# Row maxima of the first 20 units: adjacent banks, one VectorE reduction per unit

## The chip, the core and the metric

The kernel runs on one core of a Trainium2 chip. The metric is the device time of one execution in microseconds; three runs of the kernel before gave 2825.81, 2823.85 and 2824.11 us (median 2824.11). The engines are named as the profile names them: PE (TensorE), DVE (VectorE), ACT (ScalarE), POOL (GpSimd), SP (SyncE, which issues most DMAs).

## The reference, cut to what matters

Eight sequences of 1024 tokens by 256 channels pass through four residual blocks: a retention layer, a channel mix, a 16-head softmax attention with a relative bias, and the same channel mix again. The part in question is the attention:

```python
scores = jnp.einsum('bhqd,bhkd->bhqk', q, k) / np.sqrt(HEAD_DIM)   # HEAD_DIM = 16
attn = jax.nn.softmax(scores + bias[None], axis=-1)
out = jnp.einsum('bhqk,bhkd->bhqd', attn, v)
```

The kernel subtracts from the scores of each query a number that is close to the row's maximum over all 1024 keys before the exponential, so each sequence needs 16 heads x 1024 queries row maxima.

## The kernel before, in words

One sequence b follows another (the loops `for b in range(B)` in each engine's block). For each, PE runs retention, the first channel mix (q = 0 and 1, the two halves of the tokens), the projections of the attention, and then the attention itself. The second channel mix of sequence b-1 (q = 2 and 3) is laid by hand into the beginning of the attention of sequence b: that is `last_mix_and_rows` on PE (from about L748), with its counterparts on ACT (`last_mix`) and on DVE (the chain of `if u == ...` after `row_max(u)`, about L1830).

**Units.** A unit u is one head and one block of 128 queries; there are NU = 128 of them. Its scores against 1024 keys are two products of 128x512 (L882), k = 0 and 1 for the two halves of the keys. Each fills one PSUM bank (2 KiB a partition), and DVE reduces each to one maximum per query (`row_max`, L1809). After every 16 units a small reduction (L1813) joins the two halves' maxima, PE transposes them (`max_transpose`, L897), ACT negates them (L1435), and DMAs (L462) write them as an extra row of the queries' operand. Only then can the main loop multiply that block the other way round (`score_cols`, L916), with keys as rows, take exponentials (ACT, L1464), multiply the band of the bias (POOL, L2018) and weigh the values (PE, L941).

**Order of the products.** Products are numbered c. For c < 44 (2 * AHEAD, AHEAD = 22) `row_product` gives four products to two units: c = 4m is (unit 2m, k = 0), 4m+1 is (unit 2m+1, k = 0), 4m+2 is (unit 2m, k = 1), 4m+3 is (unit 2m+1, k = 1). `some_rows(1)` issues one row of two products, c = 2r and 2r+1; between the rows of `last_mix_and_rows` stand pieces of the earlier sequence's channel mix (L693, L715, L735). In the first sequence there is no earlier one and the rows follow each other.

**Banks.** For c < 40 the product goes to bank c % 4, later to bank c % 3 (`ROW_BANKS`). `score_rows` makes PE wait, before product c, until DVE has counted in `mx_r` the maximum of the last product in the same bank (`LAST_ROW[c] + 1`). PE's instructions stay in their order, so everything behind that wait waits too. `row_max(n)` makes DVE wait for `mx_s >= c + 1`, the count of finished products, before each of its two reductions.

**DVE's order around the change.** After `row_max(0)` come the statistics of the last layer norm of sequence b-1 (`ln_stats(b - 1, 5)`), after `row_max(2)` its four normalisations (L1628), after 7 and 12 the mixes of the last quarter (L1639), after 9, 10, 18 and 20 the gated outputs (L1649). PE's pieces wait for these: the transposes (L676) for the normalisations, `mix_k(b - 1, 3, ...)` (L693) for the gated output after 9, `mix_r(b - 1, 3, ...)` (L715) for the mixes after 12. When the ahead part ends, u = 22, the main loop `for s in range(NS + LAG)` starts with four more row products and four column products a step; `score_cols` waits once for 40 maxima.

Of the kernel before, what the change touches and what calls it, by code (L numbers as in the profile page):

```python
# [17 lines left out]
ALU = mybir.AluOpType  # L18
ACT = mybir.ActivationFunctionType
AX_X = mybir.AxisListType.X  # L20
# [21 lines left out]
AHEAD = 22  # L42
# [25 lines left out]
def build(nc, ins, out):  # L68
# [10 lines left out]
    NU = HEADS * NT  # L79
    NS = HEADS // 4 * 2 * NT  # L80

    with ExitStack() as ctx:
        def sb(name, shape, dt=F32):
            return ctx.enter_context(nc.sbuf_tensor(name, shape, dt))
# [6 lines left out]
        def tally(owner, name, each, step=1):  # L91
            t = Tally(sem(name), each, step)
            tallies[owner].append(t)
            return t
# [5 lines left out]
        psum = ctx.enter_context(nc.psum_tensor("psum", [P, 8, 512], F32))  # L100
# [62 lines left out]
        mx2 = sb("mx2", [P, 2, 16, 2])  # L163
# [144 lines left out]
        mx_s = tally("pe", "mx_s", 2 * NU)  # L308
        mx_r = tally("dve", "mx_r", 2 * NU)
# [24 lines left out]
        def need(eng, t, b, n):  # L334

            eng.wait_ge(t.sem, t.at(b, n))
# [28 lines left out]
        def unit(u):  # L365

            blk, ii, hh = u // 16, u % 8 // 2, u % 16 // 8 * 2 + u % 2
            return blk // 2 * 4 + hh, blk % 2 * 4 + ii, blk, hh * 4 + ii
# [42 lines left out]
        def row_product(c):  # L411

            if c < 2 * AHEAD:
                return c // 4 * 2 + c % 2, c % 4 // 2
            return c // 2, c % 2

        ROW_BANKS = [c % 4 if c < 2 * AHEAD - 4 else c % 3 for c in range(2 * NU)]
        LAST_ROW = [max((m for m in range(c) if ROW_BANKS[m] == ROW_BANKS[c]), default=None) for c in range(2 * NU)]

        def row_bank(c):  # L420

            return bank[ROW_BANKS[c]]

# [182 lines left out]
        def _(pe):  # L606
# [263 lines left out]
            def score_rows(b, c):  # L870

                u, k = row_product(c)
                h, i, _, _ = unit(u)
                if k == 0:
                    rows_wait(b, u)
                if c == 0:
                    pe.wait_ge(fn_T, 2 * norm_at(b, 3) + 2)
                if c == 3:
                    need(pe, c_lo, b, 8)
                if LAST_ROW[c] is not None:  # L880
                    need(pe, mx_r, b, LAST_ROW[c] + 1)
                pe.matmul(row_bank(c), SQ[rows_of(h, MAX_ROW), h // 2, i * P:i * P + P],  # L882
                          SK[rows_of(h, MAX_ROW), h // 2, 512 * k:512 * k + 512], start=True, stop=True)\
                    .then_inc(mx_s.sem, 1)
# [600 lines left out]
        def _(dve):  # L1485
# [145 lines left out]
            def mixes(b, q, sides=(0, 1), chunks=(0, 1)):  # L1631

                g, n, at = q % 2, norm_at(b, q % 2 + (0, 4)[q // 2]), mix_at(b, q)
                for i in sides:
                    dst, nu = ((xkT, NU_K), (xrT, NU_R))[i]
                    for c in chunks:
                        dve.wait_ge(fn_T, 2 * n + c + 1)
                        dve.wait_ge(mix_a, 4 * at + 2 * i + c + 1)
                        nc.vector.scalar_tensor_tensor(dst[:, c, :], nT[:, c, 512 * g:512 + 512 * g],  # L1639
                                                       vec[:, nu.start + c:nu.start + c + 1], dst[:, c, :],  # L1640
                                                       ALU.mult, ALU.add).then_inc(mix_b, 1)
# [71 lines left out]
            for b in range(B):  # L1713

                for t in range(NT + 1):
# [27 lines left out]
                    if 1 <= t <= NT:  # L1743
# [4 lines left out]
                        if u < NT - 1:  # L1748
                            need(dve, p_st, b, u + 1)
                            for pr in range(2):  # L1750
                                new = bank[6][:, pr * DV:pr * DV + DV]
                                if u == 0:
                                    i = nc.vector.tensor_copy(S[:, pr, :], new)
                                else:
                                    need(dve, s_upd, b, 2 * u + pr - 1)
                                    i = nc.vector.scalar_tensor_tensor(S[:, pr, :], S[:, pr, :], gamma[:, pr:pr + 1],
                                                                       new, ALU.mult, ALU.add)
# [31 lines left out]
                for n in range(8):  # L1789
# [11 lines left out]
                    if n == 7 and b > 0:  # L1801
                        mixes(b - 1, 2, (1,))

                def row_max(n):
                    for c in (2 * n, 2 * n + 1):
                        u, k = row_product(c)
                        _, _, blk, col = unit(u)
                        need(dve, mx_s, b, c + 1)
                        nc.vector.tensor_reduce(mx2[:, blk % 2, col, k:k + 1], row_bank(c), AX_X, ALU.max)\  # L1809
                            .then_inc(mx_r.sem, 1)  # L1810
                    if n % 16 == 15:
                        need(dve, mx_r, b, 2 * n + 2)
                        nc.vector.tensor_reduce(mx[:, blk, :], mx2[:, blk % 2], AX_X, ALU.max).then_inc(mx_f.sem, 1)  # L1813
# [8 lines left out]
                for u in range(AHEAD):  # L1822
                    row_max(u)
                    if b > 0:
                        if u == 0:
                            ln_stats(b - 1, 5)
                        elif u == 2:
                            ln_norms(b - 1, 5)
                        elif u == 7:
                            mixes(b - 1, 3, (0,))  # L1830
                        elif u == 9:
                            gated(b - 1, 2, (0,))
                        elif u == 10:
                            gated(b - 1, 2, (1,))
                        elif u == 12:
                            mixes(b - 1, 3, (1,))
                        elif u == 18:
                            gated(b - 1, 3, (0,))
                        elif u == 20:
                            gated(b - 1, 3, (1,))  # L1840
                u = AHEAD
                for s in range(NS + 4):
                    if s < NS:
                        while u < units[s]:
                            row_max(u)
                            u += 1
# [238 lines left out]
```

## Time and profile before

| | us |
|---|---|
| median of three runs | 2824.11 (2823.85 to 2825.81) |
| the profiled execution, its own time | 2824.51 |
| its span in the trace | 2822.7 |
| PE busy | 2696.9 (96%) |
| DVE busy | 2143.4 (76%) |
| ACT busy | 1741.6 (62%) |
| POOL busy | 1252.9 (44%) |
| mean granted clock of PE | 0.979 of full speed |

The profiled execution took 2824.51 us, 1.8 us more than the span that the trace covers, and 0.4 us more than the median. Busy shares are means over stages that have different limits; the stretches in which the first 20 units are worked on are some 40 us of each sequence's about 345 us. A clock of 1.00 in the profile is 2.4 GHz for PE and 0.50 is 1.2 GHz.

### The profile page before, as it was taken

The page shows a single profiled execution, that of the slowest core. Times are in us where ns is not written, and L with a number is a line of the kernel's source. Part 1 is how long each engine was busy: PE and PEld are TensorE (multiplying, and loading weights), DVE is VectorE, ACT ScalarE, POOL GpSimd, SP SyncE. Part 2 cuts the span into 40 slices and gives each one's busy share as a digit, 9 for nine tenths or more (in the row PEclk, how much of TensorE's full clock was granted, in tenths as well). Part 3 has the DMA queues.
Part 4 walks back from the last instruction along what each step waited for, and adds up shares of the span by engine and source line. Part 5 has one row for each costly group of instructions (what it writes and reads, how often), then busy time and mean ns, then how long its engine had stood idle before and what let it go on. Part 6 is the DMA issues. An engine that isn't in the chain of part 4 may idle for free.

```text
span 2822.7 us, 53686 instructions
## 1 busy us (share of the span) xinstructions
PE 2696.9 (96%) x19682; PEld 1476.0 (52%) x19682; DVE 2143.4 (76%) x4443; ACT 1741.6 (62%) x3671; POOL 1252.9 (44%) x1764
## 2 busy tenths in 40 slices
PE   6989999999999999999999999999999999999998
PEld 5733376433764338643486334854358533575334
DVE  5769856897569966689666996669956799567993
ACT  4428854488544884458744587536874378643885
POOL 3425544255433554335543455434454345433553
PEclk9979999999999999999999999999999999999999
DMA  6150001600015000250002400034000330003300
GB/s 193 31 126 11 24 9 34 146 17 24 9 43 137 17 24 9 57 124 17 31 1 68 113 17 31 1 89 91 17 31 13 97 72 17 31 31 93 59 2 16
DMA packets 71429, 139.18 MB, mean 49 GB/s; under 512 B 12784, under 2 KB 49696, under 8 KB 70016
## 3 DMA queue, kind: packets, MB, share of 16 engines
q1 hardware_dynamic: 69152, 135.29, 19.2%
q8 instruction: 158, 2.59, 0.4%
q14 instruction: 103, 0.84, 0.1%
q10 hardware_dynamic: 2016, 0.45, 0.1%
HBM read 86.02 MB, written 38.82 MB: 44 GB/s over the span
## 4 chain that ended last, share of the span: by engine, by line
PE 70%; DVE 17%; POOL 4%; issue 4%; ACT 2%; SPq 1%; DMA 1%; POOLq 0%; DVEq 0%; ACTq 0%
PE psum L882 18%; PE psum L941 16%; DVE mx L1809 8%; PE psum L655 7%; PE psum L1008 3%; PE psum L659 3%; PE psum L916 3%; PE psum L715 2%; PE psum L1064 2%; PE psum L977 2%; PE psum L842 2%; DVE nrm L1628 2%; POOL X L1926 1%; PE psum L1049 1%; DVE xrT L1639 1%
## 5 line engine op out<-in xcount | busy, mean ns | idle before, releaser
L1809 DVE TENSOR_REDUCE mx<-psum 128x1 f32<-128x512 f32 x2048 | 1265.5, 684 | 81.9 <-PE psum L882 81.1
L1464 ACT ACTIVATE Z<-psum 128x512 f32<-128x512 f32 x2048 | 1110.2, 598 | 273.2 <-PE psum L916 244.6
L2018 POOL TENSOR_TENSOR Z<-Z,W_low 128x256 f32<-128x256 f32 (+1 forms) x1152 | 713.2, 642 | 662.5 <-ACT Z L1464 655.5
L882 PE MATMUL psum<-SK,SQ 63*128 63x512 f32 x2048 | 761.2, 474 | 31.0 <-DVE mx L1809 26.1
L916 PE MATMUL psum<-SQ,SK 64*128 64x512 f32 x2048 | 756.3, 469 | 9.3 <-DMA SQ<-mrow 8.8
L941 PE MATMUL psum<-Z,Vx 128*17 128x256 f32 x8192 | 642.0, 388 | 0.4 <-POOL Z L2018 0.4
L882 PEld LDWEIGHTS psum<-SK,SQ 63*128 63x128 f32 x2048 | 309.0, 190 | 481.3 <-DVE mx L1809 368.0
L916 PEld LDWEIGHTS psum<-SQ,SK 64*128 64x128 f32 x2048 | 309.0, 188 | 81.4 <-ACT Z L1464 37.4
L941 PEld LDWEIGHTS psum<-Z,Vx 128*17 128x17 f32 x8192 | 138.3, 95 | 334.1 <-issue 275.6
L1926 POOL TENSOR_TENSOR X<-X,mixed 128x512 f32<-128x512 f32 x64 | 80.5, 1268 | 274.2 <-DVE mixed L1649 274.2
L1963 POOL TENSOR_TENSOR Z<-Z 128x512 f32<-128x512 f32 x64 | 82.0, 1281 | 244.5 <-DVE Z L1683 244.5
L655 PE MATMUL psum<-W_high,zT_both 128*128 128x512 f32 x384 | 166.2, 433 | 0.5 <-ACT Z L1347 0.5
L655 PE MATMUL psum<-W_low,zT_both 128*128 128x512 f32 x384 | 152.1, 396 | 0.0
L715 PE MATMUL psum<-WT,xrT 128*128 128x256 f32 x512 | 135.2, 409 | 14.0 <-DVE xrT L1639 14.0
L1385 ACT ACTIVATE Z<-psum 128x128 f32<-128x128 f32 x256 | 67.3, 277 | 107.0 <-PE psum L1064 107.0
L693 PE MATMUL psum<-xkT,WT 128*128 128x512 f32 x256 | 126.3, 612 | 5.5 <-DVE mixed L1649 3.1
L1347 ACT ACTIVATE zT_both<-psum,vec 128x128 fp32r<-128x128 f32 x128 | 51.6, 453 | 116.2 <-PE psum L649 115.6
L842 PE MATMUL psum<-nT,WT 128*128 128x512 f32 x256 | 115.8, 600 | 6.9 <-ACT nT L1294 6.6
L715 PEld LDWEIGHTS psum<-WT,xrT 128*128 128x128 f32 x512 | 98.3, 201 | 42.1 <-DVE xrT L1639 16.2
L659 PE MATMUL psum<-W_high,zT_both 128*128 128x512 f32 x384 | 120.0, 394 | 0.0
L1628 DVE TENSOR_SCALAR nrm<-X,fmv,frs 128x256 f32<-128x256 f32 x192 | 77.9, 467 | 43.7 <-POOL frs L1912 43.7
L1320 ACT ACTIVATE mixed<-psum 128x512 f32<-128x512 f32 x64 | 37.9, 594 | 117.2 <-PE psum L715 117.2
(135 smaller groups left out, 3535.9 us busy)
## 6 DMA issues: line engine op xcount, KB each, us to landing
W_low<-bias_rows SPq DMA_DIRECT2D x8, 2048.0 KB, 8.8
parts<-Z SPq DMA_DIRECT2D x32, 512.0 KB
W_low<-low_parts SPq DMA_DIRECT2D x7, 1536.0 KB, 6.7
X<-L_attn_a_x SPq DMA_DIRECT2D x8, 1024.0 KB, 5.7
SQ<-parts SPq DMA_DIRECT2D x32, 256.0 KB, 7.9
SK<-parts SPq DMA_DIRECT2D x32, 256.0 KB, 10.9
SQ<-parts SPq DMA_DIRECT2D x16, 512.0 KB, 6.6
SK<-parts SPq DMA_DIRECT2D x16, 512.0 KB, 14.6
```

What stands on the lines that cost most here:

```text
L655: pe.matmul(bank[dst], zT_parts[0][:, t % 2, c, :], Wqkvg_parts[part][:, c, c0:c0 + 512], start=c == 0 and part == 0, stop=False)
L659: mm = pe.matmul(bank[dst], zT_parts[1][:, t % 2, c, :], Wqkvg_parts[0][:, c, c0:c0 + 512], start=False, stop=c == C - 1)
L693: mm = pe.matmul(k_bank(b, q, o), WT[:, W_K, c, o * P:o * P + P], xkT[:, c, :], start=c == 0, stop=c == C - 1)
L715: mm = pe.matmul(bank[4 + pr][:, i * D:i * D + D], xrT[:, c, t * P:t * P + P], WT[:, W_R, c, :], start=c == 0, stop=c == C - 1)
L842: mm = pe.matmul(bank[QK_BANK[n % 2]], WT[:, A_Q + side, c, h * P:h * P + P], nT[:, c, 1 + 512 * g:513 + 512 * g], start=c == 0, stop=c == ...
L882: pe.matmul(row_bank(c), SQ[rows_of(h, MAX_ROW), h // 2, i * P:i * P + P], SK[rows_of(h, MAX_ROW), h // 2, 512 * k:512 * k + 512], start=T ...
L916: pe.matmul(col_bank(n), SK[rows_of(h), h // 2, j * P:j * P + P], SQ[rows_of(h), h // 2, 512 * half:512 * half + 512], start=True, stop=Tr ...
L941: mm = pe.matmul(sum_bank(s // 8)[32 * c:32 * c + HD + 1, cols], Vx[:, j, 4 * hg + c, :], ring[:, (4 * s + cols_of(s).index(c)) % RING, cols],
L1464: nc.scalar.activation(ring[:, n % RING, :], col_bank(n), ACT.Exp)\
L1628: nc.vector.tensor_scalar(nrm[:, i, :], X_of[b % 2][:, 4 * g + i, :], fmv[:, i, 0:1], frs[:, i:i + 1], ALU.subtract, ALU.mult).then_inc(fn ...
L1809: nc.vector.tensor_reduce(mx2[:, blk % 2, col, k:k + 1], row_bank(c), AX_X, ALU.max)\
L2018: nc.gpsimd.tensor_tensor(ring[:, n % RING, a:z], ring[:, n % RING, a:z], band_exp[:, 4 * hg + cols_of(s)[i], at:at + z - a], ALU.mult)\
```

## The change

For c < 40 the banks are given as 0, 2, 1, 3 by c % 4 in place of 0, 1, 2, 3. With the order of the products unchanged, the two halves of unit 2m then lie in banks 0 and 1, those of unit 2m+1 in banks 2 and 3. DVE reduces the two banks of a unit in one instruction, 128 x 2 x 512 to 128 x 2, and does so for two units at a time: nothing at even n, and at odd n, after a wait for all four products of the pair, the reduction of unit n-1 (adds 1 to `mx_r`) and that of unit n (adds 3). The other statements in DVE's order stay after the `row_max(u)` after which they stood. Units 20 and up are done as before.

```diff
-        ROW_BANKS = [c % 4 if c < 2 * AHEAD - 4 else c % 3 for c in range(2 * NU)]
+        ROW_BANKS = [(0, 2, 1, 3)[c % 4] if c < 2 * AHEAD - 4 else c % 3 for c in range(2 * NU)]
...
+                def two_units(n):
+                    need(dve, mx_s, b, 2 * n + 4)
+                    for i in range(2):
+                        _, _, blk, col = unit(n + i)
+                        nc.vector.tensor_reduce(mx2[:, blk % 2, col, :], psum[:, 2 * i:2 * i + 2, :], AX_X, ALU.max)\
+                            .then_inc(mx_r.sem, (1, 3)[i])
+
                 def row_max(n):
-                    for c in (2 * n, 2 * n + 1):
+                    if n < AHEAD - 2 and n % 2 == 1:
+                        two_units(n - 1)
+                        _, _, blk, _ = unit(n)
+                    for c in (2 * n, 2 * n + 1) if n >= AHEAD - 2 else ():
                         u, k = row_product(c)
                         _, _, blk, col = unit(u)
                         need(dve, mx_s, b, c + 1)
```

## Rows read from the trace of the kernel before

**Rows 1.** The page: the chain that ended last, by engine.

```profile
PE 70%; DVE 17%; POOL 4%; issue 4%; ACT 2%; SPq 1%; DMA 1%; POOLq 0%; DVEq 0%; ACTq 0%
```

**Rows 2.** Windows, ahead part: length, busy PE, PEld, DVE, ACT, POOL; PEclk; DMA.

```profile
1533.00:1578.00 45.00, 41.82 (x157) 22.77 (x155) 39.89 (x70) 13.30 (x23) 9.40 (x9) 1.00 0.56 144
1879.00:1924.00 45.00, 41.92 (x150) 23.16 (x148) 37.44 (x66) 11.11 (x20) 9.40 (x9) 0.92 0.50 133
```

**Rows 3.** Timeline of PE, fifth sequence: start, length, line, count, idle before it.

```profile
1536.90 0.50 PE L882 MATMUL psum<-SK,SQ 63*128 63x512 f32 x2
...
1539.68 2.00 PE L854 MATMUL psum<-WT,nT 128*128 128x256 f32 x8
...
1549.51 0.50 PE L882 MATMUL psum<-SK,SQ 63*128 63x512 f32 x2
1549.93 1.13 PE L715 MATMUL psum<-WT,xrT 128*128 128x256 f32 x4
1550.99 0.49 PE L882 MATMUL psum<-SK,SQ 63*128 63x512 f32 x2
...
1557.18 1.13 PE L693 MATMUL psum<-xkT,WT 128*128 128x512 f32 x2 [0.34 <-DVE mixed L1649]
...
1564.56 1.13 PE L715 MATMUL psum<-WT,xrT 128*128 128x256 f32 x4 [2.00 <-DVE xrT L1639]
...
1575.55 0.73 PE L882 MATMUL psum<-SK,SQ 63*128 63x512 f32 x3
```

**Rows 4.** Timeline of DVE in the same stretch.

```profile
1538.61 1.28 DVE L1809 TENSOR_REDUCE mx<-psum 128x1 f32<-128x512 f32 x2
1539.81 1.39 DVE L1617 BATCH_NORM_STATS2 fstat<-X 128x6 f32<-128x256 f32 x4
...
1541.60 2.45 DVE L1809 TENSOR_REDUCE mx<-psum 128x1 f32<-128x512 f32 x4
...
1550.04 1.29 DVE L1809 TENSOR_REDUCE mx<-psum 128x1 f32<-128x512 f32 x2 [0.20 <-PE psum L882]
...
1577.89 7.26 DVE L1809 TENSOR_REDUCE mx<-psum 128x1 f32<-128x512 f32 x12
```

**Rows 5.** Groups of DVE's instructions by line and shape: busy us, mean ns, idle before.

```profile
L1809 DVE TENSOR_REDUCE mx<-psum 128x1 f32<-128x512 f32 x2048 | 1265.5, 684 | 81.9 <-PE psum L882 81.1
...
L1726 DVE TENSOR_TENSOR Z<-psum,mask 128x512 f32<-128x512 f32 x64 | 44.2, 691 | 22.3 <-PE psum L1055 22.2
...
L1813 DVE TENSOR_REDUCE mx<-mx 128x16 f32<-128x32 f32 x64 | 11.9, 187 | 2.2
...
L1586 DVE TENSOR_REDUCE xrT<-xrT 128x16 f32<-128x512 f32 x1 | 1.0, 994 | 0.0
```

**Rows 6.** Timeline of PE's weight loads second sequence, where PE waits for a maximum.

```profile
542.03 0.18 PEld L882 LDWEIGHTS psum<-SK,SQ 63*128 63x128 f32 x1 [0.99 <-DVE mx L1809]
```

**Rows 7.** Timeline of DVE, second sequence: the reduction that this load waits for.

```profile
540.10 2.48 DVE L1809 TENSOR_REDUCE mx<-psum 128x1 f32<-128x512 f32 x4
```

**Rows 8.** Timeline of PE, sixth sequence, where its clock is low.

```profile
1880.68 0.50 PE L882 MATMUL psum<-SK,SQ 63*128 63x512 f32 x2
...
1908.34 2.07 PE L715 MATMUL psum<-WT,xrT 128*128 128x256 f32 x4 [2.00 <-DVE xrT L1639]
1910.34 0.79 PE L882 MATMUL psum<-SK,SQ 63*128 63x512 f32 x2
...
1922.49 0.73 PE L882 MATMUL psum<-SK,SQ 63*128 63x512 f32 x3
```

**Rows 9.** Timeline of PE, first sequence.

```profile
171.84 1.22 PE L882 MATMUL psum<-SK,SQ 63*128 63x512 f32 x4 [2.15 <-DMA SK<-Z]
...
182.57 0.38 PE L897 MATMUL psum<-ident,mx 128*16 128x128 f32 x1 [0.62 <-DVE mx L1813]
...
197.08 0.79 PE L916 MATMUL psum<-SQ,SK 64*128 64x512 f32 x1 [7.65 <-DMA SQ<-mrow]
```

**Rows 10.** Timeline of DVE, first sequence.

```profile
172.64 9.66 DVE L1809 TENSOR_REDUCE mx<-psum 128x1 f32<-128x512 f32 x16 [1.41 <-PE psum L882]
```

## The prediction

> **What bounds the kernel now.** The page first: PE is busy 96% of the span (the table) and holds 70% of the chain that ended last, DVE 17% [rows 1]. So time is gained or lost where PE stands still; DVE's instructions count only where PE waits for them. Next the windows around the ahead part (the 22 units before the main loop) (of sequences 4 and 5, counted from 0; the others look alike): in 45 us PE is busy 42 and DVE 37 to 40 [rows 2]. Both are nearly full there, and what holds them both full is that each runs ahead of the other across four banks.
>
> The PE timeline of the fifth sequence shows the pattern: a row of two products (L882) takes 0.43 us from its start to the next instruction's, a piece of the channel mix 1.06 us (four matmuls) or 1.92 us (eight, the row of L854), then the next row [rows 3]. No row waits for a maximum. PE's only long waits are for other results of DVE: 2.00 us before L715 for the mixes of L1639, 0.34 us before L693 [rows 3]. From row 0 at 1536.90 to row 20 at 1575.55 are 38.65 us. This sequence kept its clock (1.00). The sixth did not (0.92): after the wait of 2.00 us the piece of four matmuls takes 2.00 us in place of 1.06 [rows 2, 8]. Read in the same way, from the start of row 0 to that of row 20 (1880.68 to 1922.49 in the sixth), rows 0 to 20 take 40.52, 40.19, 41.69, 38.65, 41.81, 38.65 and 40.19 us in sequences 1 to 7, together 281.7 us.
>
> **The change: DVE's side.** Removed: 40 reductions of 512 per sequence. Added: 20 of 1024. Back to back the old ones cost 9.66 us less one tail, over 16, so 0.598 us each, with 0.085 us more until the last is complete (mean 684 ns) [rows 5, 10]. The price of 1024 elements in two banks is in no row. The slope comes from the reduction of 32 elements (187 ns) and that of 512 (684 ns): 497/480 = 1.04 ns an element, so 512 more cost 0.53 us, and one new reduction 0.598 + 0.53 = 1.13 us. Crossing a bank costs nothing visible: L1726 reads two banks with 512 elements in 691 ns [rows 5]. Bound below: two old ones less all of the small reduction's 0.187, 1.01 us. Bound above: no saving, 1.196 us, and a cost per output; L1586 has 16 outputs and takes 310 ns more than L1809, 0.02 us an output, so 1.24 us [rows 5]. I take 1.13, nearest to the slope. DVE is thus spared only 2 x 0.598 - 1.13 = 0.066 us a unit, 1.3 us a sequence.
>
> The Trainium skill's page "VectorE: DVE Perf Modes", section "The TRN2 errata — SBUF-src ops pay a fixed extra latency per instruction", puts a read of PSUM at 120 cycles plus one per element. By it a merged operation would spare 125 ns, not 66, and the sum below would be some 8 us less; no row here shows so large a fixed part between reductions that follow each other.
>
> **The change: PE's side.** Here lies the cost. Before, each of four banks came free by itself. Now DVE starts only when all four products of a pair (m) are there, and the banks come back so: product 4m+4 (bank 0) needs the pair's first reduction, 4m+5 (bank 2) needs the second, as it is the only one that brings `mx_r` on. So PE, in order, can pass 4m+5 only when both reductions are done, and with it waits the piece behind. Only what lies between row 2m+1 and row 2m+2 (call it Y) and product 4m+4 are beside the reductions. What lies between rows 2m and 2m+1 (X) is fully on the path. The loop of dependencies, from a row 2m+1:
> - to the first reduction's start: 0.53 us to the first product of a row (1549.51 to 1550.04) [rows 3, 4] and 0.1 for the second: 0.63;
> - two reductions and the tail: 2 x 1.13 + 0.085 = 2.345;
> - from the maximum to PE: product 43 waits for the third of four reductions from 540.10, which ends at 540.10 + 2 x 0.598 + 0.684 = 541.98; its weights load at 542.03 [rows 6, 7]. With rounding 0.07;
> - product 4m+5 alone until the next piece: an estimate of 0.33, a row's 0.43 less the 0.1 between its products.
>
> Sum 3.375 us plus X. Before, the same way took X + Y + 0.86. A pair so costs 2.51 - Y more: 1.45 us where Y is 1.06, 0.59 where Y is 1.92.
>
> Through one sequence: rows 0 to 1 as before, 2.35. Then nine rounds of 3.375 = 30.4 and their X: 1.92, 1.89 (transposes and a piece), 1.06, 1.06, 1.05, 1.05, 1.92, 1.18 (with the transpose of the maxima), 1.06 = 12.2. The last pair: 0.63 + 2.345 + 0.07 = 3.05 until row 20. DVE's statistics now come before the first pair; they take 1.79 us (1539.81 to 1541.60) from 1538.61, end at 1540.40, and row 1 would let it start at 1539.88: 0.5 [rows 4]. The piece `mix_k(b - 1, 3, 0)` waits for the gated output that now follows the fifth pair: 0.25. Total 48.7 us against 38.65, **10.1 us more in a sequence with full clock**. The old waits of 2.00 and 0.34 us are gone in this sum, since normalisations and mixes are ready while PE waits for banks. What was late is replaced by the second reduction of each pair.
>
> Over seven sequences: 7 x 48.7 = 341.0 less 281.7 = 59.3 us. This sum has no stretch of low clock in it. After row 20 nothing gives it back: two maxima, a gated output, two maxima take DVE 3.6 us as before, and the main loop starts with DVE as its bound, 12 reductions in a row [rows 4].
>
> **First sequence.** No pieces lie between the rows. Four products at low clock take 1.22 us [rows 9]; a pair costs 2.345 + 0.07 + 1.22 = 3.6 us against 4 x 0.598 = 2.4. Eight pairs end some 7 us late, the transpose at about 190 rather than 182.57. But the column products wait until 197.08 for the DMA of the maxima [rows 9], whose transfer stands behind earlier ones in SP's queue, so most is covered. The last pair then ends at about 197.0 and DVE has four reductions left that it had done before: 4 x 0.598 = 2.4 us. Bounds: 0 (higher clock, shorter pairs) and 7 (nothing covered). I take 2.4.
>
> POOL, ACT and SP lose and gain no instruction. POOL's squares, ACT's copies and the stores follow later by what PE is late, all with gaps of microseconds before them. The maxima's DMA of the later sequences is issued some 4 us before the column products need it.
>
> **Sum:** 2824.51 + 59.3 + 2.4 = 2886.2; the profiled execution is 0.4 above the median, within its spread, so I say 2886.5.
>
> **The rivals.**
> 1. *PE's clock falls in the new waits.* PE would stand still about 1.2 us in each round of 4.44 us (less 2 x 1.06 for the pieces, 0.43 for a row, 2 x 0.33 for the split row). For it: one wait of 2.00 us brought the clock to 0.5 in five of seven sequences [rows 8]. Against it: the 0.34 us waits did not, and each new one is under 1.1 us, in two parts. If one such stretch comes per sequence, at the mean excess of those five, 204.4/5 - 38.65 = 2.2 us, it adds 16 us: 2902. If half of each ahead part is at 1.2 GHz, pieces on the path take 2.0 for 1.06: (0.9 x 12.2 + 9 x 0.3)/2 = 6.8 us a sequence, 48 us in all: 2934.
> The Trainium skill's page "TensorE: Matmul & The Clock Gate", section "A second HAM failure mode: psum-queue depth-cycling", says that short idles between groups of matmuls, as banks are cycled, make the clock swing between its levels. That is a rule against this change; by it the second of these times is the right one, by the rows the clock holds.
> 2. *The pieces cover the reductions (faster).* If DVE's two reductions ended within Y and product 4m+4, no row would wait, and PE would be spared its waits of 2.00 and 0.34 us and the low clock behind them. 281.7 - 7 x (38.65 - 2.3) = 27 us less: 2797. It decides from the point at which two reductions together take under 0.43 + Y + 0.1 - 0.63 - 0.155, which is 1.7 us where Y is 1.92 and 0.8 where it is 1.06; the slope says 2.26. Nothing speaks for it but the four busy banks of today.
> 3. *The reductions cost less or PE's order hides more.* At 1.01 us each, 140 of them spare 17 us: 2869. At 1.24 they add 15: 2902.
>
> **How the numbers follow.** Forecast with full clock, 0.62. Rival 1, 0.25. Rival 3 beyond the forecast's own 2876 to 2896, 0.08. Rival 2, 0.03. No change (say the reductions start earlier than their wait says), 0.02. The range goes from rival 3's low end, 2868, to between rival 1's two times, 2925. A measurement of this kernel tells 0.2% (5.6 us) from no change. Faster 0.03, same 0.02, slower 0.95.
>
> **What would show it.** Group of new reductions 128x2 from 128x1024: x160, mean near 1.21 us (1.13 and its tail). PE timeline: before the second product of each even row a wait for DVE of about 0.8 us, and rounds of about 4.4 us where they took 2.98; no wait of 2.00 us before L715. Rows 0 to 20: 48.7 us. Clock near 1.00 in these windows. The main loop's steps unchanged at their own length. I am wrong if rounds stay near 3 us, if the rows do not wait for L1809's successor, or if the clock column of these windows is under 0.9.

## The result, and the profile after

The changed kernel takes 2891.51 us (median of four runs, 2891.28 to 2900.24), against 2823.98 us for the kernel before on the same chip (four runs, 2823.22 to 2825.81). The ratio is 1.0246, with a 95% interval of 1.0226 to 1.0265: slower by 68 us. The profiled execution took 2891.28 us; its span is 66.8 us longer than that of before. The forecast was 2886.5.

The page of the changed kernel: the busy time of the engines, the chain that ended last by engine, and four groups (busy us, mean ns of one, idle before it and what ended most of that).

```profile
span 2889.5 us, 53526 instructions
...
PE 2722.0 (94%) x19682; PEld 1482.9 (51%) x19682; DVE 2126.5 (74%) x4283; ACT 1741.8 (60%) x3671; POOL 1251.6 (43%) x1764
...
PE 70%; DVE 18%; issue 4%; POOL 4%; ACT 2%; SPq 1%; DMA 1%; DVEq 0%; POOLq 0%; ACTq 0%
...
L1819 DVE TENSOR_REDUCE mx<-psum 128x1 f32<-128x512 f32 x1728 | 1063.9, 685 | 37.8 <-PE psum L882 37.5
...
L882 PE MATMUL psum<-SK,SQ 63*128 63x512 f32 x2048 | 791.3, 476 | 97.2 <-DVE mx L1808 70.5
...
L1808 DVE TENSOR_REDUCE mx<-psum 128x2 f32<-128x1024 f32 x160 | 188.3, 1218 | 125.1 <-PE psum L882 125.1
...
L715 PE MATMUL psum<-WT,xrT 128*128 128x256 f32 x512 | 126.7, 389 | 0.0
```

The same group of PE's rows on the page of the kernel before:

```profile
L882 PE MATMUL psum<-SK,SQ 63*128 63x512 f32 x2048 | 761.2, 474 | 31.0 <-DVE mx L1809 26.1
```

L1808 is the new reduction, L1819 the old one, which is left for the other units. DVE has 160 instructions fewer and 17 us less to do, and PE still does the same matmuls. The two idle figures belong together: PE stood idle before its rows for 97.2 us (31.0 before), 70.5 of them until a reduction of L1808, and the new reductions stood idle for 125.1 us, all of it until a product. Each engine waits for the other in turn. L715, whose 2.00 us waits for the mixes stood in the trace before [rows 3, 8], waits for nothing now.

Timeline of PE in the changed kernel, fifth sequence: its row 0, and then one round of the pattern.

```profile
1565.35 0.50 PE L882 MATMUL psum<-SK,SQ 63*128 63x512 f32 x2
...
1578.87 0.49 PE L882 MATMUL psum<-SK,SQ 63*128 63x512 f32 x2
1579.29 1.13 PE L715 MATMUL psum<-WT,xrT 128*128 128x256 f32 x4
1580.71 0.50 PE L882 MATMUL psum<-SK,SQ 63*128 63x512 f32 x1 [0.29 <-DVE mx L1808]
1581.84 0.50 PE L882 MATMUL psum<-SK,SQ 63*128 63x512 f32 x1 [0.63 <-DVE mx L1808]
1582.27 1.13 PE L715 MATMUL psum<-WT,xrT 128*128 128x256 f32 x4
1583.33 0.50 PE L882 MATMUL psum<-SK,SQ 63*128 63x512 f32 x2
```

Timeline of DVE in the same round.

```profile
1579.43 2.36 DVE L1808 TENSOR_REDUCE mx<-psum 128x2 f32<-128x1024 f32 x2 [2.94 <-PE psum L882]
...
1583.90 2.35 DVE L1808 TENSOR_REDUCE mx<-psum 128x2 f32<-128x1024 f32 x2 [2.11 <-PE psum L882]
```

The row at 1578.87 completes a pair. Its last product is there at 1579.43; the two reductions keep all four banks until 1581.79. The next row is torn into two single products: the first gets its bank from the first reduction and waits 0.29 us, the second gets its bank from the second and starts at 1581.84, and the piece behind it starts at 1582.27. Before, a row and a piece followed each other without a wait [rows 3]. The round takes 4.46 us instead of 2.98.

Windows of the ahead part in the changed kernel, second and sixth sequences: length, busy PE, PEld, DVE, ACT, POOL; PEclk; DMA share and GB/s.

```profile
504.00:553.00 49.00, 41.31 (x140) 21.38 (x138) 33.37 (x44) 9.82 (x17) 9.15 (x9) 1.00 0.48 125
1920.00:1970.00 50.00, 42.57 (x138) 22.16 (x137) 33.26 (x43) 9.83 (x17) 9.14 (x9) 0.97 0.47 125
```

[rows 2] show windows of 45 us around the same stage; these are 49 and 50 us long. PE's busy time in them stays about 42 us, and DVE's falls from 40 or 37 to 33. Neither is full any more. By how much the stage itself grew is read from row to row, below. The clock is 1.00 in five of the seven sequences.

**Where the 66.8 us are.** From the start of row 0 to that of row 20, sequences 1 to 7 take 48.90, 48.91, 48.52, 48.89, 50.02, 48.89 and 49.78 us: 343.9 in all, 62.2 more than the 281.7 before. The same stretch of the first sequence, to its first column product, takes 40.77 us in place of 37.21: 3.56 more. Setup ahead of the first row took 1.17 us more in this execution (161.04 against 159.87 us; in the other traces of this study it takes from 158.01 to 160.99). All that lies behind row 20 (in the first sequence, behind the first column product) takes 2343.8 us together, the rest of the span, against 2343.9. The sum is 62.2 + 3.6 + 1.2 - 0.1 = 66.9. So all but 1.2 us lies in the 20 rows that the change touches (in the first sequence in them and the way to the column products), and nothing is given back behind them.

### The profile page after: what moved, and what is told of

Its sections match the earlier page's. It is cut to its first block, busy times and chain, and to the rows that moved or that the text cites. A ratio compares the mean times of both kernels' runs of the same rounds, so it can differ in the third digit from the quotient of the medians.

```text
span 2889.5 us, 53526 instructions
## 1 busy us (share of the span) xinstructions
PE 2722.0 (94%) x19682; PEld 1482.9 (51%) x19682; DVE 2126.5 (74%) x4283; ACT 1741.8 (60%) x3671; POOL 1251.6 (43%) x1764
## 4 chain that ended last, share of the span: by engine, by line
PE 70%; DVE 18%; issue 4%; POOL 4%; ACT 2%; SPq 1%; DMA 1%; DVEq 0%; POOLq 0%; ACTq 0%
PE psum L882 20%; PE psum L941 16%; PE psum L655 7%; DVE mx L1819 5%; DVE mx L1808 5%; PE psum L1008 3%; PE psum L659 3%; PE psum L916 3%; PE psum L1064 2%; PE psum L977 2%; PE psum L842 2%; POOL X L1936 1%; PE psum L1049 1%; PE psum L951 1%; DVE nrm L1628 1%
## 5 line engine op out<-in xcount | busy, mean ns | idle before, releaser
L1819 DVE TENSOR_REDUCE mx<-psum 128x1 f32<-128x512 f32 x1728 | 1063.9, 685 | 37.8 <-PE psum L882 37.5
L882 PE MATMUL psum<-SK,SQ 63*128 63x512 f32 x2048 | 791.3, 476 | 97.2 <-DVE mx L1808 70.5
L916 PE MATMUL psum<-SQ,SK 64*128 64x512 f32 x2048 | 759.2, 472 | 1.7 <-DMA SQ<-mrow 1.3
L882 PEld LDWEIGHTS psum<-SK,SQ 63*128 63x128 f32 x2048 | 319.8, 190 | 569.9 <-DVE mx L1819 313.5
L916 PEld LDWEIGHTS psum<-SQ,SK 64*128 64x128 f32 x2048 | 311.3, 188 | 72.7 <-ACT Z L1464 36.8
L1808 DVE TENSOR_REDUCE mx<-psum 128x2 f32<-128x1024 f32 x160 | 188.3, 1218 | 125.1 <-PE psum L882 125.1
L715 PE MATMUL psum<-WT,xrT 128*128 128x256 f32 x512 | 126.7, 389 | 0.0
L715 PEld LDWEIGHTS psum<-WT,xrT 128*128 128x128 f32 x512 | 93.0, 190 | 25.0 <-issue 15.1
```

What stands on the lines that cost most here:

```text
L715: mm = pe.matmul(bank[4 + pr][:, i * D:i * D + D], xrT[:, c, t * P:t * P + P], WT[:, W_R, c, :], start=c == 0, stop=c == C - 1)
L916: pe.matmul(col_bank(n), SK[rows_of(h), h // 2, j * P:j * P + P], SQ[rows_of(h), h // 2, 512 * half:512 * half + 512], start=True, stop=Tr ...
L1808: nc.vector.tensor_reduce(mx2[:, blk % 2, col, :], psum[:, 2 * i:2 * i + 2, :], AX_X, ALU.max)\
```

## The experiments

The theory: it is the wait for all four products and the coarse release of the four banks that costs, since it makes PE and DVE take turns; the wide reduction by itself saves a little. Rivals: the wide reduction or its two adjacent banks cost; the clock falls in the new waits; DVE's other work, which moved in its order, is what PE waits for.

**One wide reduction per unit, without waiting for the pair.** On the kernel before, the products are put in the order of the units, so that a unit is complete after its own row.

```diff
-            if c < 2 * AHEAD:
-                return c // 4 * 2 + c % 2, c % 4 // 2
...
-                    for c in (2 * n, 2 * n + 1):
+                    if n < AHEAD - 2:
+                        _, _, blk, col = unit(n)
+                        need(dve, mx_s, b, 2 * n + 2)
+                        nc.vector.tensor_reduce(mx2[:, blk % 2, col, :], psum[:, 2 * (n % 2):2 * (n % 2) + 2, :], AX_X, ALU.max)\
+                            .then_inc(mx_r.sem, 2)
+                    for c in (2 * n, 2 * n + 1) if n >= AHEAD - 2 else ():
```

> The kernel before, with its products in the order of the units (both halves of unit n are one row and lie in banks 0,1 or 2,3) and one reduction of 128x2x512 per unit, started after that unit's own two products; it frees two banks while the other two are filled. Theory (the cost of the change is the wait for four products and the release of the banks behind the second reduction, not the wide reduction): rows 0 to 20 about 38.7 us a sequence at full clock, no waits for DVE between rows, reductions of 1.22 us mean as after the change, time 2822 us (2812 to 2832). Rival (the wide reduction over two banks, or its two outputs, is what costs): near 2890, as after the change.

Measured: 2875.08 us (2862.05 to 2879.42), ratio 1.0172 (1.0147 to 1.0198). A miss by over 50 us. Timeline of PE in this kernel, third sequence, and windows of 4 us within the same stretch (columns as above).

```profile
875.98 0.73 PE L880 MATMUL psum<-SK,SQ 63*128 63x512 f32 x2
876.64 1.12 PE L691 MATMUL psum<-xkT,WT 128*128 128x512 f32 x2
877.70 0.73 PE L880 MATMUL psum<-SK,SQ 63*128 63x512 f32 x2
880.20 1.13 PE L713 MATMUL psum<-WT,xrT 128*128 128x256 f32 x4 [1.78 <-DVE xrT L1637]
881.26 1.22 PE L880 MATMUL psum<-SK,SQ 63*128 63x512 f32 x2
882.41 3.78 PE L713 MATMUL psum<-WT,xrT 128*128 128x256 f32 x8
```

```profile
882.00:886.00 4.00, 4.00 (x10) 2.52 (x8) 1.22 (x1) 0.60 (x1) 0.00 (x0) 0.50 0.44 182
894.00:898.00 4.00, 4.00 (x9) 2.34 (x10) 2.07 (x2) 0.00 (x0) 0.00 (x0) 0.50 0.32 57
```

No row waits for a reduction here. Two other things cost. A row of two products takes 0.66 us until the piece behind it (875.98 to 876.64) where it took 0.43 [rows 3]. And a wait for the mixes is still there, 1.78 us, after which the clock is 0.50; 14 us later it still is, with PE busy 4.00 of 4.00 us. In the second sequence, behind the same wait, the clock is back at 1.00 in the window 537 to 541 us, some 7 us after it. Rows 0 to 20 take 45.3 to 45.5 us in three sequences, 51.8 to 52.1 in three and 43.96 in the last. This run had two edits in it, order and width, so the next ones part them.

**The order alone.** The first two lines of the diff above, nothing else.

> The kernel before with only the order of the first 44 products changed (both halves of unit n in one row), reductions one product at a time. Theory: every bank still comes free by itself, so 2824 us within 4. Rival (the alternation of the two halves of PE's rows between neighbouring products is worth time in the ahead part): a row takes more than 0.43 us, 20 rows by 0.1 to 0.2 in 8 sequences, 2840 to 2856.

Measured: 2833.08 us (seven runs, 2830.62 to 2835.05), ratio 1.0032 (1.0021 to 1.0043): 9 us more, where at most 4 were said. Timeline of PE in this kernel, third sequence.

```profile
872.47 0.73 PE L880 MATMUL psum<-SK,SQ 63*128 63x512 f32 x2
873.95 1.13 PE L713 MATMUL psum<-WT,xrT 128*128 128x256 f32 x4 [0.75 <-DVE xrT L1637]
875.01 0.73 PE L880 MATMUL psum<-SK,SQ 63*128 63x512 f32 x2
875.67 1.99 PE L713 MATMUL psum<-WT,xrT 128*128 128x256 f32 x8
```

The rows cost 0.66 us here too (875.01 to 875.67), so that part of the first kernel's loss belongs to the order. But rows 0 to 20 take 41.30 us in all seven sequences, only 1.06 above the mean before, 40.24: while PE is later, the mixes are less so. The wait before L713 is 0.75 us instead of 2.00, and the clock stays up behind it. Of these 1.25 us 0.78 come from the mixes themselves, which take 1.41 us for two instead of 2.19. DVE's mixes in the kernel before, second sequence:

```profile
525.92 2.19 DVE L1639 SCALAR_TENSOR_TENSOR xrT<-nT,vec,xrT 128x512 f32<-128x512 f32 x2
```

DVE's mixes and POOL's squares in this kernel, from the timelines of these two engines, second sequence.

```profile
526.36 1.41 DVE L1637 SCALAR_TENSOR_TENSOR xrT<-nT,vec,xrT 128x512 f32<-128x512 f32 x2
...
527.12 1.54 POOL L1915 TENSOR_TENSOR Z<-Z 128x512 f32<-128x512 f32 x1 [1.53 <-ACT Z L1307]
```

The same in the kernel with one wide reduction per unit.

```profile
527.59 2.19 DVE L1637 SCALAR_TENSOR_TENSOR xrT<-nT,vec,xrT 128x512 f32<-128x512 f32 x2
...
528.11 1.12 POOL L1920 TENSOR_TENSOR Z<-Z 128x512 f32<-128x512 f32 x1 [1.53 <-ACT Z L1307]
```

Where the two overlap, one of them is longer: the square by 0.5 us in the one kernel (1.54 for 1.04), the mixes by 0.78 in the other. It is so in all seven sequences of both. Which of the two it is differs with the moment at which they meet; that the overlap is the cause was not tried by itself.

**The banks alone.** The first line of the change, without the reductions.

```diff
-        ROW_BANKS = [c % 4 if c < 2 * AHEAD - 4 else c % 3 for c in range(2 * NU)]
+        ROW_BANKS = [(0, 2, 1, 3)[c % 4] if c < 2 * AHEAD - 4 else c % 3 for c in range(2 * NU)]
```

> The kernel before with only the numbering of the banks changed (0, 2, 1, 3), reductions one product at a time. Theory: 2824 us within 4, rows 0 to 20 as before. Rival (neighbouring banks in turn for PE's writes and DVE's reads matter): more than 10 us off 2824 in either direction.

Measured: 2822.75 us (ten runs), ratio 1.0002 (0.9993 to 1.0012). Where the halves lie costs nothing.

**The change's wait, with reductions of the old width.** On the changed kernel.

```diff
-                        nc.vector.tensor_reduce(mx2[:, blk % 2, col, :], psum[:, 2 * i:2 * i + 2, :], AX_X, ALU.max)\
-                            .then_inc(mx_r.sem, (1, 3)[i])
+                        for k in range(2):
+                            ins_ = nc.vector.tensor_reduce(mx2[:, blk % 2, col, k:k + 1], bank[2 * i + k], AX_X, ALU.max)
+                        ins_.then_inc(mx_r.sem, (1, 3)[i])
```

> The changed kernel with its waits and its two counts per pair, but each unit's wide reduction done as two of 512. Theory (the waits cost, the width spares a little): a pair's reductions take 2.39 us in place of 2.26, ten rounds a sequence are 0.13 us longer, so 1.3 us a sequence and about 1 us in the first: 2891.5 + 10 = 2901 us (2897 to 2905), rows 0 to 20 about 50.2 us. Rival (the wide reduction costs): back towards 2824, below 2870.

Measured: 2907.91 us (2907.49 to 2912.63), ratio 1.0301 (1.0284 to 1.0318). Timeline of DVE in this kernel, a pair of the second sequence, and a window of its fifth.

```profile
518.55 2.48 DVE L1809 TENSOR_REDUCE mx<-psum 128x1 f32<-128x512 f32 x4 [2.94 <-PE psum L882]
```

```profile
1572.00:1626.00 54.00, 45.60 (x148) 24.49 (x147) 35.30 (x65) 11.46 (x20) 9.15 (x9) 0.94 0.46 119
```

This settles the sign of both parts. The wait and the coarse release, at the old width, make the kernel 84 us slower; wide reductions bring 16 of these back. Four old reductions take 2.48 us, two new ones 2.36: 0.12 us in each of ten pairs of eight sequences is 10 us of the 16. Rows 0 to 20 take 50.15 to 51.8 us (50.2 said). The clock is 0.94 to 0.97 in all seven sequences here, where the change kept 1.00 in five: the other 6 us, which the expectation did not have, go with these stretches of low clock. Why they are more frequent here was not tried.

**The change for half of the units.** First for units 0 to 9 only, then for 10 to 19 only (`n < 10` and `10 <= n < AHEAD - 2` in place of `n < AHEAD - 2`, in both conditions of `row_max`).

> The change for units 0 to 9 alone; units 10 to 19 in the new banks, but reduced one product at a time. Theory (a pair costs 2.51 - Y, Y being what lies between its last row and the next pair's first; old waits that it covers come off): five pairs with Y of 1.92, 1.06, 1.06, 1.06, 1.92 cost 5.5 us, 0.5 more for the statistics ahead of the first, 0.2 off for the shorter wait of the transposes: 5.9 us a sequence in sequences 1 to 7, nothing in the first, where the DMA covers it: 2824 + 41 = 2865 us; the wait of 2.00 us before L715 and the low clock behind it stay. Rival (the cost is per wide reduction or per pair, evenly): half of 67, 2857 us.

> The change for units 10 to 19 alone. Theory: five pairs with Y of 1.91 and four times 1.06 cost 6.4 us a sequence, less the wait of 2.07 us before L715, which they cover, and the 1.6 us a sequence that the low clock behind it costs on average: 2.8 us a sequence, 19 in seven, and 2 to 4 in the first sequence: 2824 + 22 = 2846 us. Rival (evenly): 2857 us.

Measured: 2868.01 us (2867.09 to 2869.31), ratio 1.0156 (1.0141 to 1.0171), and 2844.97 us (2842.40 to 2849.72), ratio 1.0071 (1.0054 to 1.0088). PE's first wait for the late mixes, from the timeline of the kernel with units 0 to 9, second sequence.

```profile
534.14 1.13 PE L715 MATMUL psum<-WT,xrT 128*128 128x256 f32 x4 [2.00 <-DVE xrT L1639]
```

The two excesses, 44.0 and 21.0 us, add up to nearly the change's 67.5. Both come out near their expectations, 2865 and 2846, and not at 2857. In the first sequence the second five pairs cost nothing (37.25 us to its first column product, 37.21 before), where 2 to 4 us were said. Five pairs cost twice as much in the first half as in the second. The second half contains the wait of 2.00 us and the low clock behind it, and with units 10 to 19 changed that wait is gone; in the first half the new waits are only added. The old wait, then, is not something that the change made shorter, but something that it hid behind its own.

**Three products, then four.** The change, with the wait split.

```diff
-                    need(dve, mx_s, b, 2 * n + 4)
                     for i in range(2):
+                        need(dve, mx_s, b, 2 * n + 3 + i)
```

> The changed kernel, with the wait for four products taken apart: the reduction of the even unit starts when three products of the pair are there, that of the odd one when all four are. Theory (the loop of dependencies of a pair runs from its last row over both reductions to the next pair's second product; its start is 0.1 us earlier): 0.1 us a pair, 1.0 a sequence, 8 in all: 2883 us (2880 to 2889). Rival (the wait for four products, and not the release of the banks, is the main cost): below 2870.

Measured: 2887.41 us (2881.44 to 2891.73), ratio 1.0229 (1.0213 to 1.0244). The runs spread over 10 us, so the time alone does not tell this kernel from the changed one. The trace does: rows 0 to 20 take 48.58 to 48.60 us in five sequences, 0.3 less than with the change. The reductions of a pair start 0.54 us after the row that completes it, where it was 0.56: at full clock the fourth product is there almost with the third, so there was next to nothing to win at the front of the pair. In the first sequence, most of it at low clock, the reductions start 0.86 us after the row and not 1.25, and the way to the first column product is 3.0 us shorter (37.75 for 40.77). Over the seven other sequences rows 0 to 20 are 1.2 us shorter together, so most of what the split wins in this stage lies in the first. PE and DVE still take turns, because the row behind a pair, and the piece behind that row, can pass only after the pair's second reduction.

**The mixes a unit earlier.** The kernel before has one real loss in this stretch, the wait of 2.00 us and the low clock behind it. Here the mixes stand after unit 11's maxima and not after 12's.

```diff
-                        elif u == 12:
+                        elif u == 11:
```

> The kernel before (neither banks nor reductions changed), with the second pair of mixes of L1639 after row_max(11) in place of row_max(12) in DVE's order. Theory (the kernel before loses, at the one wait of 2.00 us before L715 and in the low clock behind it, about 2.0 + 1.6 us a sequence in sequences 1 to 7, which the change covers): rows 0 to 20 about 36.7 us in place of 40.2 on average, clock 1.00 in these windows, time 2824 - 25 = 2799 us (2794 to 2812). Rival (the wait only moves to the rows, whose maxima come later by the two mixes): 2820 to 2824.

Measured: 2806.87 us (2802.25 to 2809.02), ratio 0.9935 (0.9922 to 0.9947). Timelines of PE: the row and the piece that had waited, second sequence; then the fifth sequence's first column product, and the first of its second block of queries.

```profile
524.64 0.49 PE L882 MATMUL psum<-SK,SQ 63*128 63x512 f32 x2
525.06 1.13 PE L715 MATMUL psum<-WT,xrT 128*128 128x256 f32 x4
...
1566.15 0.46 PE L916 MATMUL psum<-SQ,SK 64*128 64x512 f32 x1
...
1589.33 0.49 PE L916 MATMUL psum<-SQ,SK 64*128 64x512 f32 x1 [0.23 <-DMA SQ<-mrow]
```

The wait is gone, the clock holds, and rows 0 to 20 take 36.34 to 36.83 us in every sequence (forecast 36.7). Of the 25.7 us won there 11.2 are lost again: from the first column product to the next sequence's row 0 it takes 0.2 to 2.6 us more in sequences 1 to 6, and 3.7 more from there to the end of the last. All idle time before L916 that a DMA ended, of PE's matmuls and of its weight loads together, so that one wait can count twice, from the view of that line in this kernel (us, times):

```profile
  DMA SQ<-mrow: 34.9, 23
```

In the kernel before it is 22.9 us, 13 times. Of the matmuls alone it is 13.9 us here, 7 times, and 8.8 us there, 3 times, so PE waits 5 us more, not 12. These waits are new in sequences 3 to 7, and all five stand where 1589.33 stands: before the first product of the second block. The low clock lasts longer too, 8.5 us over the stages behind the rows in these seven sequences, which accounts for some 4 us more at half the speed (an estimate); in the last sequence such a stretch follows the longest of the waits, 2.54 us. The column products come earlier than the maxima's row of the operand, whose DMAs stand in SP's queue behind the store of the sequence before.

**The same, for the kernel with one reduction per unit.** The first experiment's diff and this one's.

> Products in the order of the units, one wide reduction per unit, and the mixes after row_max(11). Theory (that kernel's cost without the earlier mixes was 0.23 us a row, since two products of one unit lie in the same half of PE's rows, and a clock that fell behind the wait for the mixes): no low clock, rows 0 to 20 about 38.65 - 2.3 + 20 x 0.23 = 40.9 us, time about 2828 us (2820 to 2835). Rival (the wide reductions themselves bring the clock down or cost time): above 2860.

Measured: 2827.00 us (ten runs, 2826.18 to 2828.56), ratio 1.0009 (1.0000 to 1.0018). Rows 0 to 20 take 40.45 to 40.49 us in all seven sequences, with no low clock and no wait. So of the first experiment's 51 us, 48 went with the late mixes: the wait and the long stretches of low clock behind it. What still parts it from the kernel with the mixes alone moved is the order: 40.47 less 36.57 is 3.9 us a sequence for 20 rows, near the 0.23 us a row seen in the timeline, and 27 us in seven sequences. The times, 2827.00 and 2806.87 us, are only 20 us apart, since this kernel does not lose the 11.2 us behind the rows. The wide reductions on adjacent banks do no harm once nothing waits for a pair of units.

**The store later in SP's queue.** If the maxima's DMAs wait behind the store, it should stand behind them. First with the mixes a unit earlier, then by itself.

```diff
-                        if b > 0:
-                            store(b - 1)
+                    if blk == 1 and b > 0:
+                        store(b - 1)
```

> The kernel before, with the mixes after row_max(11) (the run that came out at 2806.9 us, whose rows 0 to 20 took 36.6 us but whose main loop took 1.2 us longer a sequence and waited for the DMA of the maxima 23 times in place of 13) and the two stores of the finished sequence issued by SP after the maxima of block 1 in place of before them. Theory (the stores of 1 MB stand in front of the second block's maxima in the DMA queues, and the ahead part that is now shorter runs into that): the 1.2 us a sequence come back, main loop to the next row 0 about 303 us, 2806.9 - 8 = 2799 us (2794 to 2804). Rival (the wait is for the loads of the heads 8 to 15, which are 1.5 MB and stay where they are): 2805 to 2809.

> The kernel before with only the stores issued after block 1's maxima. Theory: its ahead part is long enough for the queue to drain, so nothing waits: 2824 us within 4. Rival (the same wait costs something there too): 2815 to 2819.

Measured: both together 2798.89 us (2797.95 to 2800.06), ratio 0.9909 (0.9894 to 0.9924); the store alone 2824.44 us (eleven runs), ratio 0.9999 (0.9990 to 1.0008). The page of the kernel with both, and its view of L916.

```profile
span 2796.9 us, 53686 instructions
...
PE 71%; DVE 16%; POOL 4%; issue 3%; ACT 2%; SPq 2%; DMA 1%; POOLq 0%; DVEq 0%; ACTq 0%
...
L882 PE MATMUL psum<-SK,SQ 63*128 63x512 f32 x2048 | 759.6, 473 | 31.2 <-DVE mx L1809 26.2
```

```profile
  DMA SQ<-mrow: 23.4, 13
```

The waits for the DMA are back near their old sum (23.4 for 22.9 us; of the matmuls alone 9.1 for 8.8), the later stages at their old length, and rows 0 to 20 keep 36.3 to 36.8 us. This kernel is the fastest of the study: 26 us under the one before and 93 under the changed one, with every reduction at its old width. By itself the store's place is worth nothing: in the kernel before, all three waits of PE's column products for this DMA lie in the first sequence, so in the others PE gets to them too late to meet the store.

## Why the prediction was right, step by step

**What bounds the kernel: right.** DVE lost 17 us of work and the kernel became 68 us slower. It was PE's idle time before its rows that grew, from 31.0 to 97.2 us. The width of the reductions counted only where PE waited for them: at the old width, in the same wait, the kernel took 16 us more.

**The new reduction: right.** Mean 1218 ns where 1.21 us was said; two with their tail take 2.35 to 2.36 us (2.345 said). The second starts 1.14 us after the first (2.36 less 1.22), where 1.13 was said. Against four old ones in 2.48 us they spare 60 ns a unit (66 said), so [rows 5]'s slope held across two banks. The 125 ns that followed from the Trainium skill's page "VectorE: DVE Perf Modes", section "The TRN2 errata — SBUF-src ops pay a fixed extra latency per instruction", is not what these reductions show: two old ones back to back are 1.196 us, and one new one is 1.14.

**PE's loop of a pair: right in sum, with two terms off against each other.** Said: 0.63 to the reduction's start, 2.345, 0.07 to PE, 0.33 for the lone product, 3.375 in all. Measured in the round shown: 0.56, 2.36, 0.05 and 0.43, 3.40. The lone product costs as much as a whole row (0.43 us from 1581.84 to 1582.27, and a row 0.42 from 1578.87 to 1579.29), so at full clock the two products of a row overlap nearly entirely. The fourth product then adds almost nothing at the front of the pair, and the wait for three and then four brought 0.3 us a sequence and not 1. That the two errors, 0.07 too much and 0.10 too little, nearly cancel is luck. The round is 4.46 us (about 4.4 said). Before the second product the wait reads 0.63 us where 0.8 was said; the idle time is counted from the first product's modelled end at 0.50 us, not from 0.33.

**Rows 0 to 20: 0.2 us short.** Said 48.7; five sequences took 48.52 to 48.91, two took 50.02 and 49.78 with a clock of 0.97 in the sixth. Timeline of PE in the changed kernel, sixth sequence, with its row 20:

```profile
1936.59 0.50 PE L882 MATMUL psum<-SK,SQ 63*128 63x512 f32 x1 [0.63 <-DVE mx L1808]
1937.02 1.96 PE L715 MATMUL psum<-WT,xrT 128*128 128x256 f32 x4
...
1970.13 0.73 PE L882 MATMUL psum<-SK,SQ 63*128 63x512 f32 x3 [1.42 <-DVE mx L1808]
```

Right after one of the waits of 0.63 a piece of four matmuls took 1.96 us for 1.13. Over seven sequences this makes 62.2 us in place of 59.3: 0.6 from the five, 2.4 from the two.

**The first sequence: 3.56 in place of 2.4.** The step that was off is how late the transpose of the maxima comes. Timelines of PE in the changed kernel, first sequence, from its row 0:

```profile
161.04 0.51 PE L882 MATMUL psum<-SK,SQ 63*128 63x512 f32 x2 [0.53 <-DMA SK<-Z]
...
187.89 1.22 PE L882 MATMUL psum<-SK,SQ 63*128 63x512 f32 x3 [0.34 <-DVE mx L1808]
...
191.56 0.79 PE L882 MATMUL psum<-SK,SQ 63*128 63x512 f32 x1 [0.34 <-DVE mx L1808]
192.28 0.38 PE L897 MATMUL psum<-ident,mx 128*16 128x128 f32 x1
192.59 0.79 PE L882 MATMUL psum<-SK,SQ 63*128 63x512 f32 x2
...
195.86 1.22 PE L882 MATMUL psum<-SK,SQ 63*128 63x512 f32 x3 [0.34 <-DVE mx L1808]
199.53 1.22 PE L882 MATMUL psum<-SK,SQ 63*128 63x512 f32 x3 [2.45 <-DVE mx L1808]
...
201.81 0.76 PE L916 MATMUL psum<-SQ,SK 64*128 64x512 f32 x1
```

A pair at low clock takes 3.67 us (3.6 said); the first two rounds, all or mostly at full clock, take 2.98 and 3.18, and the one that has the transpose in it takes 4.30, which the forecast left out. The nine rounds together take 32.5 us, and nine times 3.6 are 32.4, so the price of a pair held. But the transpose comes 31.24 us after row 0 (161.04 to 192.28), where it came 22.70 us after it (159.87 to 182.57): 8.5 us late and not the 7 that the forecast took for eight pairs (190 for 182.57). Eight pairs of 1.2 us more would be 9.6; how it came from there to 7 the forecast does not say. From the transpose on it had 9.4 us to the first column product, and 9.53 came. That the remaining four old reductions come uncovered after the last pair was right: 199.53 to 201.81.

**Setup: not in the sum.** 1.17 us before the first row, where the change has no instruction. The first row starts between 158.01 and 161.04 us in the thirteen traces of this study, so it is most likely one execution against another.

**What goes late next, and what gives nothing back: right.** The late mixes no longer hold PE up, and the stages behind row 20 have, taken together, their old length to 0.1 us.

**Rival 1, the clock: not borne out at its size.** Five of seven sequences kept 1.00; where it fell it cost 1 us a sequence. Of the two times under this rival the rule of the Trainium skill's page "TensorE: Matmul & The Clock Gate", section "A second HAM failure mode: psum-queue depth-cycling", which has the clock swing with such short idles, pointed to 2934; two idle stretches of 0.29 and 0.63 us in every round of 4.46 did not bring that about here. Why it fell in the sixth and the eighth sequence was not tried. **Rivals 2 and 3**: the reductions of a pair are never covered, and cost what the slope said.

In sum (us over the kernel before): 59.3 + 2.4 was said, 62.2 + 3.6 + 1.2 - 0.1 came, 5 us more in 67.

## What to carry to other kernels

Merging two instructions saves their fixed part (60 ns here, 1.2 us a sequence), and it changes when work may start and when buffers come free: count the semaphore's increments and ask how many of the ring's buffers stand still while the merged instruction runs. Here it was the whole ring, four of four banks, and the alternation cost 10.9 us a sequence (51.1, the mean with old reductions in the same wait, less 40.2), net of the old wait and low clock that it hid, against the 1.2 saved. If two engines keep each other fed through a ring, a merge should leave buffers free beside it: with one unit per reduction two of four banks stayed free, and no row waited. One free bank was not tried. Merging on an engine that does not bound the stage had at best these 1.2 us to win; looking for the one long wait in the same timeline (2.00 us for a late operand, one line moved) brought 17 us, and 26 together with the DMA that it uncovered.

## What the runs showed of the hardware that was not expected

- **Two products of the same unit cost more than two of different units.** A row of two 63x128 by 63x512 products takes 0.43 us until the next piece when they belong to two units, and 0.66 when they belong to one unit, at full clock; it is the main difference between the two kernels with the earlier mixes, whose rows 0 to 20 are 3.9 us apart. The operands of neighbouring units lie in different halves of the partitions; that the two halves of PE's rows work side by side is the reading that fits, argued and not shown.
- **A clock once lowered may stay low under full load.** After one wait of 1.78 us, PE worked 4.00 of 4.00 us at 0.50, and did so still 14 us later; in another sequence of the same kernel it was back at 1.00 some 7 us after the same wait. What decides between the two was not tried. Behind the waits of 0.75 us it stayed at 1.00 in all seven sequences, and with the change's own 0.29 and 0.63 us in five of seven.
- **Work of DVE and of POOL is longer where the two overlap.** Two mixes of 128x512 take 1.41 us, and 2.19 us when POOL's square of 128x512 starts 0.52 us into them; in another order, where it starts 0.76 us into them, it was the square that grew, from 1.04 to 1.54 us, and the mixes kept their 1.41.
